# A fused attention and FFN kernel: two of six parts of the bias addition go from VectorE to GpSimd, a group's last two weight blocks are loaded from SyncE's queue, and one pair of score blocks changes its place on TensorE

## The reference

```python
x = hidden                                  # 8 batches x 256 tokens x 512, fp32
qkv = layernorm(x) @ w_qkv                  # 32 query heads, 8 key/value heads, D = 128
scores = q @ k^T * D**-0.5 - slope(head) * sqrt(distance), masked above the diagonal
x = x + softmax(scores) @ v @ w_o
y = layernorm(x)
hit = softmax(y @ centroids^T / 0.1) > 0.01
x = x + where(hit_row(y) & hit_column, y @ w_ffn^T + b_ffn, 0)
```

## Time and profile before

| | |
|---|---|
| median of 3 runs | 1273.97 us (1272.35 to 1277.04) |
| the profiled execution | 1272.32 us, of which the span of its instructions is 1270.7 us |
| PE busy | 1238.5 us, 97% of the span |
| DVE, ACT, POOL busy | 787.2, 751.9, 520.2 us |
| mean granted clock of TensorE | 0.996 |
| PE's idle time that ended with POOL's ring | 15.8 us in 15 places |

### The profile page before, as it was taken

The page is one execution under the profiler, slowest core; times in us unless marked ns, Lnnn a source line. Parts: engine busy times, 40 slices in busy tenths (PEclk is TensorE's granted clock), DMA queues, the critical chain, the costliest instruction groups (busy, mean ns, idle before and its releaser), DMA issues.

```text
span 1270.7 us, 21113 instructions
## 1 busy us (share of the span) xinstructions
PE 1238.5 (97%) x5880; PEld 1029.3 (81%) x5880; DVE 787.2 (62%) x2086; ACT 751.9 (59%) x2171; POOL 520.2 (41%) x476
## 2 busy tenths in 40 slices
PE   9899999999999999999999999999999999999988
PEld 8688878887788878887888878888788878888777
DVE  7777656566555565656565566555655566668577
ACT  5776566565555656665556656664566566556443
POOL 4422636226342545226352455325452364233213
PEclk9899999999999999999999999999999999999999
DMA  5543535444453444444443444534444444523203
GB/s 199 178 132 123 161 119 182 140 135 142 152 173 123 141 160 154 157 140 132 165 155 118 161 160 149 166 124 149 142 155 149 138 160 154 168 83 116 92 9 133
DMA packets 205530, 180.71 MB, mean 142 GB/s; under 512 B 12096, under 2 KB 158784, under 8 KB 205504
## 3 DMA queue, kind: packets, MB, share of 16 engines
q1 hardware_dynamic: 199680, 162.04, 38.8%
q0 software_dynamic: 5824, 18.36, 4.9%
HBM read 101.45 MB, written 78.91 MB: 142 GB/s over the span
## 4 chain that ended last, share of the span: by engine, by line
issue 34%; PE 31%; POOL 21%; DVE 5%; ACT 4%; DMA 4%; POOLq 1%; SPq 0%; DVEq 0%; ACTq 0%
PE ps L1385 29%; POOL ring L592 11%; POOL wqkv_lo L551 2%; POOL wo_lo L551 2%; POOL v_lo L598 2%; POOL wqkv_hi L549 2%; ACT prob L765 1%; DMA vT<-turned_s 1%; PE ps L1405 1%; DMA turned<-ring_whole 1%; POOL wo_hi L549 1%; ACT prob L777 1%; POOL raw L557 1%; POOL raw L560 1%; DVE vT L1083 1%
## 5 line engine op out<-in xcount | busy, mean ns | idle before, releaser
L1385 PE MATMUL ps<-xnT,wqkv_hi 128*128 (+2 forms) x1560 | 483.3, 391 | 1.7 <-DVE kT L1005 1.3
L592 POOL TENSOR_TENSOR ring<-ring_whole,pT_hi 128x512 fp32r<-128x512 f32 x189 | 246.1, 1302 | 522.3 <-ACT pT_hi L756 522.0
L1385 PEld LDWEIGHTS ps<-xnT,wqkv_hi 128*128 128x128 f32 x1560 | 289.2, 188 | 67.4 <-DVE kT L1005 6.1
L1385 PE MATMUL ps<-xnT,wqkv_lo 128*128 (+1 forms) x780 | 303.3, 389 | 0.0
L765 ACT ACTIVATE prob<-prob,negmax 128x256 f32<-128x256 f32 (+1 forms) x384 | 177.1, 463 | 187.5 <-DVE negmax L1083 187.5
L1385 PE MATMUL ps<-wo_hi,oT_hi 128*128 128x512 f32 x512 | 200.1, 391 | 0.8 <-DVE acc L1062 0.8
L1385 PE MATMUL ps<-wo_lo,oT_hi 128*128 128x512 f32 x512 | 199.6, 390 | 0.0
L1385 PE MATMUL ps<-wo_hi,oT_lo 128*128 128x512 f32 x512 | 199.2, 389 | 0.0
L756 ACT ACTIVATE pT_hi<-ring_whole 128x512 fp32r<-128x512 f32 x189 | 118.0, 625 | 129.9 <-DMA ring_whole<-turned 88.3
L1062 DVE TENSOR_TENSOR acc<-ps,acc 128x512 f32 (+1 forms) x128 | 88.2, 690 | 146.6 <-PE ps L1385 146.2
L1385 PEld LDWEIGHTS ps<-xnT,wqkv_lo 128*128 128x128 f32 x780 | 146.9, 188 | 30.8
(11 more groups left out here) (155 smaller groups left out, 1788.4 us busy)
## 6 DMA issues: line engine op xcount, KB each, us to landing
turned<-ring_whole SPq DMA_DIRECT2D x189, 256.0 KB, 2.1
ring_whole<-turned SPq DMA_DIRECT2D x189, 256.0 KB, 2.9
turned_v<-vT SPq DMA_DIRECT2D x32, 256.0 KB, 2.0
turned_s<-prob SPq DMA_DIRECT2D x32, 256.0 KB, 2.0
prob<-turned_s SPq DMA_DIRECT2D x32, 256.0 KB, 2.7
turned_s<-vT SPq DMA_DIRECT2D x32, 256.0 KB, 2.0
vT<-turned_s SPq DMA_DIRECT2D x32, 256.0 KB, 3.8
vT<-turned_v SPq DMA_DIRECT2D x31, 256.0 KB, 2.7
```

The lines of the kernel that those rows point to most:

```text
L592: pool.tensor_tensor(ring_slot(c), whole_slot(c), pT_hi[:, c % 2, :].bitcast(F32), ALU.subtract).then_inc(pT_lo_done, 1)
L1385: ins = pe.matmul(dst, l, r, start=start and m == 0, stop=stop and m == n - 1)
```

## The change

Three things are changed.

1. Parts 2 and 5 get their bias on POOL: `sum_scores(u, b)` is one add of 128x512 in place, and DVE then takes the negated maximum of all four heads in one `tensor_reduce` (`find_max`). `exps` reads these parts with scale 1.0. On POOL `sum_scores(u, 0)` stands behind `v_lo_part(u)`, and `sum_scores(u-1, 1)` between `pT_lo_part(u, 1)` and `pT_lo_part(u, 2)`. On DVE `find_max(u-1, 1)` stands behind `turn(u-1, 3)` and `turn(u-1, 4)` of step i = 1, where `add_bias(u-1, 5)` stood at i = 0; `invert_sums(u-1, 3)` goes from the end of i = 1 to the start of i = 2, and `turn(u-1, 5)` from i = 2 to i = 3.
2. The w_qkv blocks 2 and 3 of the next group are loaded from SP's queue in the group's last unit (`last_qkv`, each behind a wait for one of POOL's splits, around `scores_in(v, 0)`), no longer by POOL within `split_qkv`. `raw_loaded` is counted anew.
3. `scores(u, 0, 0)` and `scores(u, 0, 1)` go behind `project_out(u, 1)` on PE, and their two `add_bias` behind `add_out(u, 1)` on DVE. Beside that, ACT takes `pT_hi_part(1, 0)` ahead of two exponentials in unit 1, and behind the last unit chunks 1 and 2 one place earlier each; there DVE no longer starts with the wait for part 5.

```diff
             def turn_first(v):
                 scores_out(v, 0)
                 scores_in(v, 0)
+                turn_rest(v)
+
+            def turn_rest(v):
                 scores_out(v, 1)
...
+            def last_qkv(g, c):
+
+                sp.wait_ge(raw_split, g * (2 * NC) + c - 1)
+                rows = w_qkv[c * P:(c + 1) * P, :]
+                kv = rows[:, NH * D:].rearrange("p (a n) -> p a n", a=2)[:, :, bass.ds(g * D, D)]
+                sp.dma_start(raw[:, c % 2, 0:HPG * D], rows[:, bass.ds(g * (HPG * D), HPG * D)]).then_inc(last_loaded[c % 2], 16)
+                sp.dma_start(raw[:, c % 2, HPG * D:QKV_W].rearrange("p (a n) -> p a n", a=2), kv).then_inc(last_loaded[c % 2], 16)
+
+            def unit(v):
+                turn_v(v)
+                turn_first(v)
+                turn_second(v)
+
+            def last_of_group(g):
+                v = g * QUADS + QUADS - 1
+                turn_v(v)
+                scores_out(v, 0)
+                last_qkv(g + 1, 2)
+                scores_in(v, 0)
+                last_qkv(g + 1, 3)
+                turn_rest(v)
+                turn_second(v)
 
...
-            with sp.Fori(1, UNITS - 3) as v:
-                turn_v(v)
-                turn_first(v)
-                turn_second(v)
+            for v in range(1, QUADS - 1):
+                unit(v)
+            last_of_group(0)
+            with sp.Fori(1, NKV - 1) as g:
+                for q in range(QUADS - 1):
+                    unit(g * QUADS + q)
+                last_of_group(g)
...
                 for c in range(NC):
                     if c == 2:
                         v_lo_part(g * QUADS - 1)
-
-                    pool.wait_ge(raw_loaded[c % 2], g * 96 - 96 + 32 * (c // 2 + 1))
+                        sum_scores(g * QUADS - 1, 0)
+
+                    if c < 2:
+                        pool.wait_ge(raw_loaded[c % 2], g * 64 - 32)
+                    else:
+                        pool.wait_ge(last_loaded[c % 2], g * 32)
                     split(raw[:, c % 2, :], wqkv_hi[:, c, :], wqkv_lo[:, c, :], g * (2 * NC) + SETUP + c + 1)
-                    if c < 2:
-                        load_after(g, c)
...
+            def sum_scores(u, b):
+
+                pool.wait_ge(s_in[b], u * 16 + 16)
+                pool.wait_ge(bias_ready, group_count(u))
+                by_head = score_tile(b).rearrange("p (i h c) -> p h i c", i=P // BLK, h=HPG)
+                pool.tensor_tensor(by_head, by_head, bias[:, :, P:SEQ].rearrange("p h (i c) -> p h i c", c=BLK),
+                                   ALU.add).then_inc(scores_summed, 1)
+
+            def pT_lo_first(u):
+                pT_lo_part(u, 0)
+                pT_lo_part(u, 1)
+                sum_scores(u - 1, 1)
+                pT_lo_part(u, 2)
...
             def plain_body(u):
-                for c in range(CHUNKS):
+                pT_lo_first(u)
+                for c in range(3, CHUNKS):
                     pT_lo_part(u, c)
                 v_lo_part(u)
+                sum_scores(u, 0)
...
                     pT_lo_part(u + 1, h)
+                    if h == 1:
+                        sum_scores(u, 1)
...
-                    ins = act.activation(s, s, ACT.Exp, bias=negmax[:, n:n + 1], scale=-1.0, accum_out=rowsum[:, n:n + 1])
+                    ins = act.activation(s, s, ACT.Exp, bias=negmax[:, n:n + 1], scale=1.0 if e % 3 == 2 else -1.0,
+                                         accum_out=rowsum[:, n:n + 1])
...
+                    if is_second(u):
+                        pT_hi_part(u, 0)
                     exps(u - 1, 3)
                     exps(u - 1, 4)
-                    pT_hi_part(u, 0)
+                    if not is_second(u):
+                        pT_hi_part(u, 0)
                 for i in range(PROJ_OUTS + lag - 2):
...
             pT_hi_part(u, 0)
+            pT_hi_part(u, 1)
             normalise(u - 1, 2)
             exps(u - 1, 5)
-            pT_hi_part(u, 1)
+            pT_hi_part(u, 2)
             normalise(u - 1, 3)
             oT_hi_part(u, 0)
-            pT_hi_part(u, 2)
             pT_hi_part(u, 3)
...
+            def find_max(u, b):
+
+                dve.wait_ge(scores_summed, u * 2 + b + 1)
+                n = 4 * (2 * b + 1)
+                dve.tensor_reduce(negmax[:, n:n + HPG], score_tile(b).rearrange("p (i h c) -> p h i c", i=P // BLK, h=HPG),
+                                  AX_XY, ALU.max, negate=True).then_inc(scores_biased, 1)
...
                         invert_sums(u - 1, 2)
-                        add_bias(u - 1, 5)
+                    if attn and i == 2:
+                        invert_sums(u - 1, 3)
...
                             turn(u - 1, 3)
                             turn(u - 1, 4)
-                            invert_sums(u - 1, 3)
-                        if i == 2:
+                            find_max(u - 1, 1)
+                        if i == 3:
                             turn(u - 1, 5)
...
-                if p is None:
-                    add_bias(u, 0)
-                    add_bias(u, 1)
-                    invert_sums(u, 0)
...
+                add_bias(u, 0)
+                add_bias(u, 1)
                 if p == 0:
                     dense_part(p, source, 1)
-                if p is not None:
-                    invert_sums(u, 0)
+                invert_sums(u, 0)
                 add_out(u, 2)
                 turn_scores(u, 1)
                 turn(u, 0)
                 turn(u, 1)
-                add_bias(u, 2)
+                find_max(u, 0)
...
-            add_bias(u - 1, 5)
             dense_part(1, 1, 0)
             invert_sums(u - 1, 2)
             dense_part(1, 1, 1)
+            find_max(u - 1, 1)
...
-                if p is None:
-                    scores(u, 0, 0)
-                    scores(u, 0, 1)
                 if p is not None:
...
-                if p is not None:
-                    scores(u, 0, 0)
-                    scores(u, 0, 1)
+                scores(u, 0, 0)
+                scores(u, 0, 1)
```

More of the change, by code:

```diff
@@ L12 @@
 AX_X = mybir.AxisListType.X
+AX_XY = mybir.AxisListType.XY
 P = 128
@@ L208, in build @@
         s_in = [sem("s_in0"), sem("s_in1")]
+        scores_summed = sem("scores_summed")
         scores_biased = sem("scores_biased")
@@ L499, in _ @@
             turn_second(0)
-            with sp.Fori(1, UNITS - 3) as v:
-                turn_v(v)
-                turn_first(v)
-                turn_second(v)
+            for v in range(1, QUADS - 1):
[5 more added lines that the diff above has]
+                last_of_group(g)
+            unit(UNITS - QUADS)
             sp.wait_ge(qkv_mm, PROJ_OUTS * (UNITS - QUADS + 1))
@@ L603, in plain_body @@
             def plain_body(u):
-                for c in range(CHUNKS):
+                pT_lo_first(u)
+                for c in range(3, CHUNKS):
                     pT_lo_part(u, c)
                 v_lo_part(u)
+                sum_scores(u, 0)
             def group(g, last):
                 u = g * QUADS
-                for c in range(3):
-                    pT_lo_part(u, c)
+                pT_lo_first(u)
                 pool.wait_ge(scores_biased, g * (BIASED * QUADS))
@@ L635, in group @@
                 v_lo_part(u + 1)
+                sum_scores(u + 1, 0)
                 plain_body(u + 2)
                 if not last:
-                    for c in range(CHUNKS):
+                    pT_lo_first(u + 3)
+                    for c in range(3, CHUNKS):
                         pT_lo_part(u + 3, c)
@@ L667, in _ @@
                     v_lo_part(0)
+                if h == 3:
+                    sum_scores(0, 0)
                 split_o(0, h)
@@ L676, in _ @@
                 v_lo_part(u)
-            for c in range(CHUNKS):
+                sum_scores(u, 0)
+            pT_lo_first(QUADS - 1)
+            for c in range(3, CHUNKS):
                 pT_lo_part(QUADS - 1, c)
@@ L704, in _ @@
                     pT_lo_part(UNITS, j - 1)
+                if j == 1:
+                    sum_scores(UNITS - 1, 1)
             for p in range(2, QUADS):
```

27 lines of the change are left out of this document (9 added, 18 removed).

## The result

| | before | changed |
|---|---|---|
| median of the runs on the same chip | 1274.25 us (4 runs) | 1311.28 us (4 runs, 1309.63 to 1314.92) |
| ratio | 1 | 1.0293, 95% interval 1.0262 to 1.0323 |
| profiled execution and its span | 1272.32, 1270.7 us | 1314.92, 1313.3 us |
| mean granted clock of TensorE | 0.996 | 0.983 |

The account below looks back on a forecast made before the run. PE was taken to bound the kernel, busy 1238.5 of 1270.7 us. The terms 9.1 + 14.7 - 5.5 + 11.0 - 4.7 = +24.6 us, on 1273.97, gave 1298.5 us, range 1278 to 1316.

Parts of the forecast that it names:

- What bounds the kernel: PE, busy 1238.5 of 1270.7 us: any new PE wait counts in full, and taking work from DVE by itself gains nothing.
- The bias of part 5, where it stands: ACT stands 3.0 us at exps(u-1, 5) for find_max with its list behind it, so chunks 2 and 5 come late.
- plain units: 13 units (3, 6, 7, 10, 11, to 27) lose 0.7 us each at chunks 2 and 5: +9.1 us.
- Second units: Seven units (5 to 29), where POOL also splits w_o, lose 2.1 us each at chunk 2: +14.7 us.
- First units: Seven first units of a group: old waits and late releases go (-11.5), 0.85 us each comes instead: -5.5 us.
- Units with a layer norm: PE waits longer for the layer norm's transposes: 3.0 us in units 1, 2, 30, 2.0 in 31: +11.0, bounds 6 and 15.
- rival D: Heavier, chance 0.15: new 2 us waits lower PE's clock, eleven units lose some 1.6 us more each: 1315 us.
- Weights from SP: Loading w_qkv blocks from SP's queue, its waits covered, costs 0; without the cover up to 3 us a group.
- Scores behind `project_out(u, 1)`: Scores come 2.7 us later on PE but are covered: 0; without that cover each unit would lose up to 0.5 us.
- The tail: Behind the last unit, PE's wait of 2.75 us and most of 2.12 go: -4.7 us, bounds 2.7 and 6.5.

Follow-up runs that it names:

- the six of 1.71 and 1.72 set by hand: Kernel before, with PE made to stand at the start of six plain units until POOL has run seven steps: 1285.73 us, ratio 1.0109.
- the tail's own experiment: Kernel before with only the tail's order changed: hi parts of chunks 0 and 1 before the exponentials, add_bias(u-1, 5) behind the second dense_part: 1269.91 us, ratio 0.9946.

## Why the prediction was near, and where it was off

**What bounds the kernel** held: all that was lost was lost on PE, and DVE's relief (787 to 723.5 us busy) did not help. But the forecast counted waits and late releases alone. PE's idle time is only 22.6 of the 42.6 us. The other 20.0 are matmuls that took longer, 12.6 of it in the slow groups counted above.

**The bias of part 5, where it stands** was right in mechanism and size: ACT's stand 2.89 where 3.0 was forecast in unit 18, plain units +0.65 on average where +0.7 was, shown to be ACT's list by moving one call. One remark hid more than it said: turns 3 and 4 "are over by 675.61 and don't matter". They were over at that point of the unit, 10.0 us in, in both kernels, but only 0.2 us ahead of the sum. With the sum moved to the front alone, they held the maximum, and it came just 0.3 us sooner. That is why both had to move.

**Second units** of the loop were 2.0 us late at chunk 2, 1.83 of it a wait, as forecast (2.1). The term was under-sized by what follows: in three of six the next seven or eight matmuls ran at half the clock, some 1.5 us more each. Unit 29 itself lost only 1.0.

**First units** came near by luck, since two errors cancel. In the kernel before, the seven together were 17.8 us longer than seven times 35.56, where I had counted 11.5 us to gain; in the changed kernel they are 14.0 us longer, where I had 6.0. The old wait at chunk 0 went, and one at chunk 5 came that I had at some 0.5 us with its late release and that was 1.1 to 1.6 us long. Unit 8 of the changed kernel, SP's issues, ACT, PE:

```profile
332.71 0.33 SPq L431 DMA_DIRECT2D turned<-ring_whole  x1
336.01 0.36 SPq L436 DMA_DIRECT2D ring_whole<-turned  x1
```
```profile
338.89 0.63 ACT L814 ACTIVATE pT_hi<-ring_whole 128x512 fp32r<-128x512 f32 x1 [5.06 <-DMA ring_whole<-turned]
```
```profile
340.99 0.49 PE L1443 MATMUL ps<-pT_hi,v_hi 128*128 128x512 f32 x1 [1.31 <-POOL ring L623]
```

The way out took 3.3 us instead of the median of 2.1, beside two w_o loads of POOL that are issued from 332.03 on; that these slowed it is likely but was not tested. I had reckoned with a DMA that is a little quicker than the median.

**Units with a layer norm** is the term that was furthest off: +23.8 instead of +11.0, above even the upper bound of 15. In unit 1 PE waited 3.25 us for the low part of a query projection, and in unit 30 2.50 for the transposes:

```profile
52.23 1.22 PE L1443 MATMUL ps<-xnT,wqkv_hi 128*128 128x512 f32 x2 [3.25 <-DVE qT_lo L1070]
...
1161.22 1.11 PE L1463 MATMUL ps<-ident,prob 128*128 128x128 f32 x4 [2.50 <-DVE prob L1055]
```

The waits themselves were sized well: PE's idle time in these units grows by 2.5, 3.4, 2.6 and 2.9 us, 11.5 in all, though unit 1's longest wait is not the one that I had named. What the term lacks is the clock. Units 1 and 2 have 31 slow matmuls instead of 8, 4.6 us more, and units 30 and 31 have 26 where they had none, 5.1 us more, eight of them behind the wait ahead of unit 30 that the forecast had not. That is 9.7 of the 23.8 us; the remaining 2.6 are late releases and the like.

**The clock** I had as rival D and at nothing in the forecast, and this is the step that failed in size: 12.6 us. The truth lies between the two: not all eleven units, but half of the second units of the loop and all four with a layer norm. My argument against D took the wrong wait of the earlier trace rows. Behind the one of 2.12 us the clock stayed, but behind that of 2.75, three matmuls on, twelve matmuls take 4.51 us, and the granted clock is 0.52:

```profile
1209.63 4.51 PE L1385 MATMUL ps<-xnT 128*128 128x512 f32 x12
```
```profile
1209.80:1213.00 3.20, 3.20 (x9) 2.49 (x9) 1.54 (x4) 3.20 (x14) 0.97 (x1) 0.52 0.00 0
```

**Weights from SP: 0** was misleading as a reason. The move did not cost, but without it the changed kernel is 16 us slower: the add in `split_qkv` and the loads can't both be in POOL's queue for nothing. I costed two edits at nothing, one of which was the other's cover.

**Scores behind `project_out(u, 1)`: 0** was right within 2 us. **The tail, -4.7** was right as a number (-5.0) and in part by luck. The wait of 2.75 us went, as forecast, but of the 2.12 us only 1.2 went, where I had nearly all. The eight slow matmuls behind the wait of 2.75 went as well, 1.5 us that I did not have.

## What to carry to other kernels

When an input of a queue comes later, cost the stand of the consumer's whole list. Then look for a place in that list behind which nothing urgent stands: one call moved here was worth 28 us, and the add and its maximum moved together 56. Work handed to another engine needs its place in three queues at once; half of such a move can be worse than none (+72 us). Put the clock into every estimate in which TensorE gets new waits of some 2 us, with its own chance, and look at the matmuls behind the waits that the old trace already has. And check a sum by its terms: two of those here were near only because errors in them cancelled.

## What the runs showed of the hardware

The same wait does not always bring the lower clock. Windows of the changed kernel, columns as in the earlier trace rows: unit 1 from 51 on as there, then 2.5 us behind the waits at chunk 2 of units 17 and 13, and 3 us around unit 30's wait:

```profile
51.00:57.00 6.00, 4.77 (x11) 3.84 (x12) 3.37 (x7) 3.14 (x13) 2.50 (x2) 0.51 0.35 123
667.80:670.30 2.50, 2.50 (x8) 2.03 (x9) 2.23 (x4) 2.50 (x6) 2.42 (x3) 0.73 0.02 7
519.80:522.30 2.50, 2.48 (x11) 2.07 (x12) 2.20 (x4) 2.50 (x6) 2.42 (x3) 1.00 0.01 6
1161.00:1164.00 3.00, 2.78 (x9) 2.39 (x10) 3.00 (x7) 0.60 (x1) 0.00 (x0) 0.50 0.31 87
```

In units 17 and 13 PE had waited the same 1.83 us at the same instruction, and the clock was 0.73 after one and 1.00 after the other; units 9, 17 and 25 show it, units 5, 13 and 21 do not. Behind the four waits of 2.5 us and more of this kernel the clock was at or near 0.50, the level of 1.2 GHz (0.50 to 0.59 in windows of 3 to 6 us).

The other runs widen the doubtful stretch on both sides. With DVE's places moved alone, PE waits 2.54 to 2.57 us at the same place of 21 units; the clock fell behind 15 of these waits and stayed at 1.00 behind 6. The windows behind two of them:

```profile
941.30:943.80 2.50, 2.50 (x11) 2.04 (x12) 2.36 (x5) 2.50 (x11) 0.42 (x1) 1.00 0.20 75
979.75:982.25 2.50, 2.50 (x8) 1.98 (x9) 2.36 (x5) 2.50 (x11) 0.42 (x1) 0.68 0.20 75
```

With the loads back on POOL in the changed kernel, it fell behind 4 of 7 waits of 1.73 to 1.75 us, while behind the six of 1.71 and 1.72 set by hand it stayed. In the changed kernel even the wait of 1.63 us ahead of unit 30 has eight slow matmuls behind it. Behind all 23 waits of 2.7 us and more that the traces here show from 50 us on, it fell. What decides between 1.6 and 2.6 us is open.

POOL's add of 128x512 with four-level patterns on both sources took 1.28 to 1.31 us wherever it stood in the changed kernel. DVE's maximum took 0.69 us from `vT` and 0.65 from `prob`, and none of its 64 rows was stretched, as the addition was that met POOL; of the four instructions of the addition in the tail's own experiment two took 1.36 and 1.37 us.
